# Third layer: step size in the exponent of the decays within chunks, the plain transposed tile by ScalarE, the decays over the sum by broadcast DMA

## The reference, cut to what matters

```
proj = x @ W_in.T + b_in;  gate, hBC, dt = split(proj)
hBC = silu(conv4(hBC));  h, B, C = split(hBC)
dt = softplus(dt + dt_bias);  h = h * dt;  Adt = -exp(A_log) * dt
A_cum = cumsum(Adt within a chunk)
M = (C B^T) * exp(A_cum[l] - A_cum[s]),  s <= l
Y_diag = M @ h
states = recurrence over chunks of (B * exp(A_cum[-1] - A_cum))^T h
Y_off = (C @ states) * exp(A_cum)
y = Y_diag + Y_off + D * hBC_h;  g = y * silu(gate)
out = rmsnorm(g) * norm_w @ W_out.T + b_out
```

## Time and profile before

| what | value |
|---|---|
| median of three runs | 1292.9 us (1292.6 to 1293.01) |
| the profiled execution's own time | 1296.16 us |
| its span | 1294.4 us |
| mean granted TensorE clock | 0.961 |
| busy: TensorE matmul, VectorE, ScalarE, GpSimd | 89%, 73%, 61%, 44% of the span |
| preparation of the third layer's mixer | about 597 to 655 us from the span's start |
| its loop, first to last L1606 | 667.1 to 1103.7 us |

### The profile page before, as it was taken

One profiled execution on the slowest core, in us unless ns is written; L12 is line 12 of the kernel. 1 busy time (PEld: TensorE's weight loads), 2 busy tenths in 40 slices (PEclk: granted clock), 3 DMA queues, 4 the chain that ended last, 5 costly groups with the idle time before them and its releaser, 6 DMA issues.

```text
span 1294.4 us, 14453 instructions
## 1 busy us (share of the span) xinstructions
PE 1150.9 (89%) x4948; PEld 615.3 (48%) x4948; DVE 939.9 (73%) x1361; ACT 795.5 (61%) x1089; POOL 573.9 (44%) x310
## 2 busy tenths in 40 slices
PE   5777999999989999998489999999999999797887
PEld 1332344444344444444266666666666666322554
DVE  4667999999955545345689999998999999323354
ACT  4567666767543334226668888888888888335542
POOL 9002899898816756230014544554454455300000
PEclk8889999999989999898699999999999999798999
DMA  3001555555422111100000000000000000000000
GB/s 121 1 1 58 192 197 178 191 180 180 174 105 82 50 41 41 41 21 0 2 15 15 15 21 15 15 22 15 15 14 22 16 15 8 1 0 1 1 1 33
DMA packets 31111, 68.48 MB, mean 53 GB/s; under 512 B 6101, under 2 KB 12022, under 8 KB 30774
## 3 DMA queue, kind: packets, MB, share of 16 engines
q1 hardware_dynamic: 31038, 67.56, 16.1%
HBM read 65.25 MB, written 1.51 MB: 52 GB/s over the span
## 4 chain that ended last, share of the span: by engine, by line
PE 41%; DVE 30%; ACT 15%; issue 7%; POOL 6%; DMA 1%; DVEq 0%; SPq 0%; POOLq 0%; ACTq 0%
DVE work L1542 7%; DVE work L1561 6%; DVE work L656 4%; PE ps L1006 4%; PE ps L1196 4%; PE ps L1022 3%; PE ps L1014 3%; POOL work L717 3%; ACT work L1403 3%; DVE yd L1606 3%; ACT work L1398 3%; PE ps L1237 2%; DVE work L1609 2%; PE ps L437 2%; ACT ps L553 2%
## 5 line engine op out<-in xcount | busy, mean ns | idle before, releaser
L1670 POOL TENSOR_TENSOR ssum<-ssum,rs 128x1024 f32<-128x1024 f32 x32 | 77.1, 2410 | 221.3 <-DVE work L1542 219.0
L656 DVE TENSOR_TENSOR_SCAN work<-ps,work 128x1024 f32<-128x1024 f32 x64 | 146.6, 2291 | 8.3
L1542 DVE SCALAR_TENSOR_TENSOR work<-work,w_t 128x1024 f32<-128x1024 f32 x96 | 123.3, 1285 | 24.0 <-ACT work L1403 21.7
L437 PE MATMUL ps<-work,ident 128*128 128x512 f32 x256 | 121.7, 598 | 5.6 <-POOL work L717 5.4
L996 POOL TENSOR_TENSOR work<-work,ssum 128x1024 f32<-128x1024 f32 x32 | 76.2, 2388 | 110.1 <-DVE work L1085 57.7
L1085 DVE TENSOR_TENSOR work<-work,ps 128x512 f32<-128x512 f32 x64 | 43.8, 687 | 99.8 <-PE ps L1014 99.8
L553 ACT ACTIVATE ps<-work,A 128x1024 f32<-128x1024 f32 x64 | 71.6, 1118 | 72.4 <-DVE work L656 72.3
L1064 ACT ACTIVATE work<-ps 128x512 f32<-128x512 f32 x64 | 38.1, 597 | 115.4 <-PE ps L1006 115.4
L717 POOL TENSOR_TENSOR work<-work 128x1024 f32<-128x1024 f32 x42 | 99.1, 2362 | 13.6 <-DVE work L656 12.3
L1678 POOL TENSOR_TENSOR yd<-yd,work 128x896 f32<-128x896 f32 x32 | 67.1, 2097 | 70.7 <-DVE work L1609 70.7
L1585 DVE SCALAR_TENSOR_TENSOR work<-work,ps 128x64 f32<-128x64 f32 x384 | 79.4, 275 | 6.3
(11 more groups left out here) (347 smaller groups left out, 2587.5 us busy)
## 6 DMA issues: line engine op xcount, KB each, us to landing
work<-bc_rows SPq DMA_DIRECT2D x42, 512.0 KB, 3.5
yd<-bc_rows SPq DMA_DIRECT2D x22, 512.0 KB, 3.6
...
shared<-in_f SPq DMA_DIRECT2D x3, 512.0 KB, 6.1
...
```

Of the source, the lines that this page charges most:

```text
L437: mm = pe.matmul(ps[:, YACC + h, :], ident[:, :], HS[u % 4][:, h * BL:(h + 1) * BL], start=(n == 0), stop=(n == DS - 1))
L656: dve.tensor_tensor_scan(h, flat_pair(DABANK), h, 0.0, ALU.mult, ALU.add).then_inc(m0["scan"], 1)
L1542: c = dve.scalar_tensor_tensor(HC[u], HP[:, tap:tap + SEQ], par(u, "taps", tap), HC[u], ALU.mult, ALU.add)
L1670: pool.tensor_tensor(ssum[:, b, :], ssum[:, b, :], rs[:, :, :].rearrange("p k t -> p (k t)"), ALU.add).then_inc(m2["ss"], 1)
```

## The change

1. The factor DT of `HDT` goes into the exponent. `LNDT` = ln(DT + 1e-30) is made by ScalarE (one Ln of 128x512). The transposed sums of the start get a second set of 32 rows: ln(DT) minus the cumulative sum, from two more matmuls per chunk (`LNDT` by the identity, `ADT` by `fall`). The set is split into three bf16 parts like the first (64 partitions at a time); the negated copy goes away. The exponentials within chunks then give the decay times the step size. The clamp at 1.0 in `mask_and_weigh` becomes one at 1e30.
2. `HDT` is now the plain transposed tile; ScalarE copies it out of PSUM (`turned_out`, two copies of 128x512 within `exponentials`), and VectorE's `weigh` makes `HDD` alone.
3. `spread_sums` and `decays_out` go away. At the start ScalarE takes exp of the sums (`decay_rows`, 32x512, four times), SP stores them to DRAM (`sdo_rows`) and loads each head's row broadcast over its 64 partitions into Y (`load_decays`, two DMAs of 64x896 per tile). The bf16 parts go through DRAM as well (`arg_rows`), which makes three DMAs of `load_rows` out of four.

The diff, without declarations of semaphores and lines that only build or clear constants (`fall` is minus `upper`, `tiny` is 1e-30, `sel2` is gone):

```diff
@@ -139,16 +139,19 @@
         zero = sb("zero", [P, P])
+        fall = sb("fall", [P, P])
+        parts_lo = sb("parts_lo", [2 * H2, T], BF16)
+        LNDT = sb("lndt", [P, NT, H2])
         sel = selectors[0:96, :, :]
-        sel2 = sb("sel2", [96, H2, P2], BF16)
         eps_t = sb("eps_t", [P, 1])
+        tiny = sb("tiny", [P, 1])
@@ -222,6 +225,8 @@
         share_rows = nc.dram_tensor("share_rows", [E, T], F32, kind="Internal").ap()
+        arg_rows = nc.dram_tensor("arg_rows", [2 * H2, 3, T], BF16, kind="Internal").ap()
+        sdo_rows = nc.dram_tensor("sdo_rows", [H2, T], F32, kind="Internal").ap()
@@ -1123,7 +1128,7 @@
         BT, GT = tiles(5), tiles(6)
-        nparts = slot(7)[0:96, 0:T // 2].bitcast(BF16)
+        split = [parts[0:2 * H2, :], slot(7)[0:2 * H2, 0:T // 2].bitcast(BF16), parts_lo[:, :]]
@@ -1169,25 +1174,57 @@
                 here = slice(b * SEQ, (b + 1) * SEQ)
+                rows = (m2["rows0"], m2["rows1"])[n % 2]
+                pair = arg_rows[H2 + 2 * t:H2 + 2 * t + 2, :, here].rearrange("h k (c l) -> (h k) c l", l=P)
+                sp.dma_start(arg_w[ROW0:ROW0 + 6, n % 2, :, :], pair).then_inc(rows, 16)
                 for h in range(2):
-                    of_head = slice(2 * t + h, 3 * H2, H2)
-                    r = ROW0 + 3 * h
-                    rows = (m2["rows0"], m2["rows1"])[n % 2]
-                    sp.dma_start(arg_w[r:r + 3, n % 2, :, :], nparts[of_head, here].rearrange("k (c l) -> k c l", l=P)).then_inc(rows, 16)
-                    sp.dma_start(arg_m[r + 6:r + 9, n % 2, :, h, :], parts[of_head, here].rearrange("k (c l) -> k c l", l=P)).then_inc(rows, 16)
+                    r = ROW0 + 6 + 3 * h
+                    sp.dma_start(arg_m[r:r + 3, n % 2, :, h, :], arg_rows[2 * t + h, :, here].rearrange("k (c l) -> k c l", l=P)).then_inc(rows, 16)
+            def store_rows(b):
+                sp.wait_ge(m2["dve"], m2["parts"] + (b + 1) * NB // BATCH)
+                here = slice(b * SEQ, (b + 1) * SEQ)
+                for k in range(3):
+                    sp.dma_start(arg_rows[:, k, here], split[k][:, here]).then_inc((m2["rows_out0"], m2["rows_out1"])[b], 16)
+            def store_decays(b):
+                sp.wait_ge(m2["sdo"], (b + 1) * NB // BATCH)
+                here = slice(b * SEQ, (b + 1) * SEQ)
+                sp.dma_start(sdo_rows[:, here], rtf[0:H2, here]).then_inc((m2["rows_out0"], m2["rows_out1"])[b], 16)
+            def load_decays(n):
+                b, t = divmod(n, CT)
+                if n >= 2:
+                    sp.wait_ge(m2["outp"], n - 1)
+                    sp.wait_ge(m2["sqr"], n - 1)
+                for h in range(2):
+                    sp.dma_start(Y[n % 2][h * P2:(h + 1) * P2, P:],
+                                 sdo_rows[2 * t + h:2 * t + h + 1, b * SEQ + P:(b + 1) * SEQ].to_broadcast([P2, SEQ - P])).then_inc(
+                                     (m2["sdo_in0"], m2["sdo_in1"])[n % 2], 16)
             load_tile(1)
+            store_rows(0)
+            store_decays(0)
             sp.wait_ge(m2["rows_const"], 1)
-            sp.wait_ge(m2["act"], m2["neg"] + NB)
+            sp.wait_ge(m2["rows_out0"], 64)
             load_rows(1)
+            store_rows(1)
+            store_decays(1)
+            load_decays(0)
+            load_decays(1)
+            sp.wait_ge(m2["rows_out1"], 64)
             for n in range(CT * BATCH - 2):
+                if n >= 1:
+                    load_decays(n + 1)
                 load_rows(n + 2)
+            load_decays(CT * BATCH - 1)
@@ -1205,7 +1242,7 @@
                 if 0 in quarters:
-                    pe.wait_ge((m2["rows0"], m2["rows1"])[u], 64 * (n // 2 + 1))
+                    pe.wait_ge((m2["rows0"], m2["rows1"])[u], 48 * (n // 2 + 1))
@@ -1222,14 +1259,6 @@
 
-            def spread_sums(n, b, t):
-
-                pe.wait_ge(m2["L"], 4 * n + 4)
-                for h in range(2):
-                    mm = pe.matmul(ps[:, BACK + h, :], sel2[:, 2 * t:2 * t + 2, :].rearrange("k a p -> k (a p)"),
-                                   parts[:, b * SEQ + h * BL:b * SEQ + (h + 1) * BL], start=True, stop=True)
-                mm.then_inc(m2["sdo_mm"], 1)
-
@@ -1245,7 +1274,7 @@
             def within_chunks(n):
-                pe.wait_ge(m2["sdo"], n + 1)
+                pe.wait_ge(m2["hdt"], 2 * n + 2)
@@ -1324,8 +1352,13 @@
             pe.wait_ge(m2["bc_pad"], 2 * NB)
+            pe.wait_ge(m2["act"], m2["lndt"] + 1)
+            pe.wait_ge(m2["rows_const"], 1)
             for i in range(NT):
-                mm = pe.matmul(ps[0:H2, 4 + i // 4, (i % 4) * P:(i % 4 + 1) * P], ADT[:, i, :], upper[:, :], start=True, stop=True)
+                here = slice((i % 4) * P, (i % 4 + 1) * P)
+                pe.matmul(ps[0:H2, 4 + i // 4, here], ADT[:, i, :], upper[:, :], start=True, stop=True)
+                pe.matmul(ps[H2:2 * H2, 4 + i // 4, here], LNDT[:, i, :], ident[:, :], start=True, stop=False)
+                mm = pe.matmul(ps[H2:2 * H2, 4 + i // 4, here], ADT[:, i, :], fall[:, :], start=False, stop=True)
@@ -1410,6 +1442,13 @@
 
+            def turned_out(n, k):
+                act.wait_ge(m2["hdd"], 2 * n + k + 1)
+                if k == 0 and n >= 1:
+                    act.wait_ge(m2["ydiag"], n)
+                act.activation(HDT[:, k * BL:(k + 1) * BL], ps[:, FRONT + k, :], ACT.Copy).then_inc(m2["hdt"], 1)
@@ -1417,6 +1456,8 @@
                         act.activation(ST[:, 0, :], four(MID)[:, 0, :], ACT.Copy).then_inc(m2["first_state"], 1)
+                    if q >= 2:
+                        turned_out(n, q - 2)
@@ -1426,18 +1467,15 @@
 
-            def decays_out(n, u):
-                act.wait_ge(m2["sdo_mm"], n + 1)
-                if n >= 2:
-                    act.wait_ge(m2["outp"], n - 1)
-                    act.wait_ge(m2["sqr"], n - 1)
-                act.activation(Y[u][:, P:], flat2(BACK)[:, P:], ACT.Exp).then_inc(m2["sdo"], 1)
-
                 act.activation(rs[:, :, :], wide(Y[u]), ACT.Square).then_inc(m2["sqr"], 1)
+            def decay_rows(k):
+                act.wait_ge(m2["mid"], k + 1)
+                act.activation(blk(rtf[0:H2, :], k), ps[0:H2, 4 + k, :], ACT.Exp).then_inc(m2["sdo"], 1)
@@ -1450,19 +1488,19 @@
             act.activation(ADT, ADT, ACT.Ln, bias=1.0).then_inc(m2["act"], 1)
+            act.wait_ge(m2["dve"], m2["dt"] + 1)
+            act.activation(LNDT[:, :, :], DT, ACT.Ln, bias=tiny[:, :]).then_inc(m2["act"], 1)
             act.activation(CDEC, ps[:, 2, :].rearrange("p (i h) -> p i h", h=H2), ACT.Exp).then_inc(m2["act"], 1)
-            for k in range(NB):
-                act.wait_ge(m2["pe"], m2["cumT"] + 1)
-                act.activation(blk(parts[0:32, :], k), ps[0:H2, 4 + k, :], ACT.Copy).then_inc(m2["act"], 1)
-                act.wait_ge(m2["mid"], k + 1)
-                act.activation(blk(parts[32:64, :], k), part_tmp[0:H2, k % 2, :], ACT.Copy).then_inc(m2["act"], 1)
+            act.wait_ge(m2["pe"], m2["cumT"] + 1)
+            for k in range(NB):
+                act.activation(blk(split[0], k), ps[0:2 * H2, 4 + k, :], ACT.Copy).then_inc(m2["act"], 1)
+                if k >= 1:
+                    decay_rows(k - 1)
+            decay_rows(NB - 1)
             pad_h(0, 0)
-            for k in range(NB):
-                act.wait_ge(m2["dve"], m2["parts"] + k + 1)
-                act.activation(blk(nparts, k), blk(parts, k), ACT.Copy, scale=-1.0).then_inc(m2["act"], 1)
@@ -1472,7 +1510,6 @@
             def step(n, b, t, u):
-                decays_out(n, u)
@@ -1526,13 +1563,12 @@
             for k in range(NB):
-                r, tb = rs[0:H2, k % 2, :], part_tmp[0:H2, k % 2, :]
-                dve.wait_ge(m2["act"], m2["hi_mid"] + 2 * k + 1)
-                own(dve.tensor_tensor(r, ps[0:H2, 4 + k, :], blk(parts[0:32, :], k), ALU.subtract))
-                dve.tensor_copy(tb, r).then_inc(m2["mid"], 1)
+                r = rs[0:2 * H2, k % 2, :]
+                dve.wait_ge(m2["act"], m2["hi"] + k + 1)
+                own(dve.tensor_tensor(r, ps[0:2 * H2, 4 + k, :], blk(split[0], k), ALU.subtract))
+                dve.tensor_copy(blk(split[1], k), r).then_inc(m2["mid"], 1)
                 dve.wait_ge(m2["mid"], k + 1)
-                dve.wait_ge(m2["act"], m2["hi_mid"] + 2 * k + 2)
-                dve.tensor_tensor(blk(parts[64:96, :], k), r, tb, ALU.subtract).then_inc(m2["dve"], 1)
+                dve.tensor_tensor(blk(split[2], k), r, blk(split[1], k), ALU.subtract).then_inc(m2["dve"], 1)
@@ -1565,9 +1601,7 @@
                 product(HDD, DEC, 0, m2["hdd"])
-                product(HDT, DT, 0, m2["hdt"])
                 dve.wait_ge(m2["tr"], 2 * n + 2)
-                product(HDT, DT, 1, m2["hdt"])
@@ -1604,7 +1638,7 @@
                 dve.scalar_tensor_tensor(YD[:, :], HC[u], vec[:, VCOL["d2"] + t:VCOL["d2"] + t + 1], flat2(BACK), ALU.mult, ALU.add).then_inc(m2["yd"], 1)
-                dve.wait_ge(m2["sdo"], n + 1)
```

(5 more changed lines are left out.)

24 lines of the change are left out of this document (12 added, 12 removed).

## The result

| | before | after |
|---|---|---|
| median of the runs | 1293.0 us (1292.6 to 1295.9, 5 runs) | 1299.7 us (1298.7 to 1300.4, 5 runs) |
| profiled execution, its span | 1296.16, 1294.4 us | 1298.69, 1297.0 us |
| loop, first YD to last YD | 436.60 us | 445.95 us |
| one of the 28 plain tiles, YD to YD, mean | 14.02 us | 14.33 us (13.96 to 14.86) |
| tile 0, tile 16, last interval | 15.73, 16.50, 11.76 | 15.95, 16.94, 11.76 |

The ratio is 1.0041 with a 95% interval of 1.0023 to 1.0059. The prediction was 1282.1 us, in a range of 1277 to 1288, with a chance of 0.93 of faster; it was wrong in sign and by 17.6 us.

The account below looks back on a forecast made before the run. Two nearly level rings of waits, one through VectorE, TensorE and ScalarE, were taken to bound the kernel; loop -11.5 and way in +0.7 gave -10.8, so 1292.9 - 10.8 = 1282.1 us, range 1277 to 1288.

Parts of the forecast that it names:

- The queue of SP: SP's DMAs in the loop: five a tile become six, everything lands within 8 us, so costed at nothing.
- The landing time: Loop DMAs: the nearest row, a 512 KB broadcast, lands in 3.6 us; the two new broadcasts are 458 KB together.
- The slower rival: In the loop, Y* waits for the late broadcast of the decays: +50 us, 1343; chance 0.03.
- The loop's two rings: Chains of waits through VectorE and through TensorE, again level at 13.6 to 13.7 us a tile; loop -11.5 us.
- The rival of dear copies: ScalarE's copies in the loop take 0.69 us each, a tile 13.9, in all 1289 us; chance 0.07.
- The rival of the lower clock: TensorE falls to 1.2 GHz in the loop, standing still before project_h: more than 200 us; chance 0.01.
- The way in: Preparation ahead of the loop: +3.9 us for matmuls, -3.2 for what follows, +0.7 us in sum.
- The 48 matmuls of the sums: TensorE's cumulative sums at the start: 16 become 48, only neighbours overlap, 7.6 us, +3.9.
- The rule of the Trainium skill: No overlap among the start's matmuls, since all use the same rows: +7.4 for +3.9, 1285.6 us; chance 0.14.
- The split: Splitting the sums into three bf16 parts at the start: 8.06 us instead of 11.04, -3.0.
- The transposes: TensorE's transposes at the end of the way in: reached after 8.8 us instead of 9.0.
- tile 0's own step: Before the 31 intervals: tile 0's convolution no longer waits 0.76 us for pad_h, -0.76 us.

Follow-up runs that it names:

- experiment 1: Changed kernel with load_tile(n + 2) put ahead of load_decays(n + 1) in SP's loop, nothing else: 1275.1 us, ratio 0.9826.
- experiments 1 and 2: The second of these: changed kernel with load_tile behind the same wait for sum_out but ahead of the two broadcasts: 1274.5 us, ratio 0.9812.
- experiment 4: Changed kernel with a third broadcast of 64x896, into a place that nobody reads, ahead of load_tile: 1366.0 us, ratio 1.0538.
- experiment 7: Experiment 1 with ScalarE's order changed, first_state ahead of the third exponential: 1277.2 us, ratio 0.986.
- experiment 6: Kernel before with only HDT by ScalarE's copies (turned_out) instead of VectorE's two products; spread_sums and decays_out stay: 1304.9 us, ratio 1.0064.

## Why the prediction was wrong, step by step

**The queue of SP: this step failed.** The prediction said "The weights are wanted by project_h 18 us after that wait" and costed the new order at nothing. The 18 us count one tile too many. `load_decays(n + 1)` waits for the `sum_out` that ends 0.9 us behind YD of tile n; `load_tile(n + 2)` behind it serves `project_h(n + 2)`, which stands at the **start** of step n + 1, 5.28 us after the same YD. The weights are wanted 4.4 us after the wait, not 18. The order needs 1.15 us of issue, 3.6 to 4.5 us of landing and 0.14 us, so 4.9 to 5.8: it is short by 0.5 to 1.4, and the plain tiles are 0.85 us longer in the mean than in experiment 1, 28 times. What hid the load before was that it was issued one period earlier, at 5.64 us after YD (915.33 against 909.69). Its use came at 5.93 us after the next YD, 14.03 + 5.93 - 5.64 = 14.3 us later. The prediction wrote down that the load would be "issued now some 11 us later", and did not ask what was left of 14.3. The subtraction leaves 3.3 us for a landing that takes 3.6 or more.

**The landing time.** I took one for all: "the nearest row, a broadcast of 512 KB, lands in 3.6 us". That was near for the broadcasts (3.7; the two are 448 KB in the page's count, not 458), but the load was taken as independent of what stands ahead of it. It lands in 2.4 or 2.5 us with no broadcast ahead (experiments 1 and 2), in 4.0 behind two, 4.1 behind one and 4.4 behind three. DMA: Bandwidth & Descriptors (Queues, rings and completion order) in the Trainium skill says that SP's queue has one ring on each of the DMA engines, and that each engine consumes descriptors in the order of its ring. By that rule a load behind a broadcast would start later. The landing times bear this out in direction. Their sizes do not grow with the bytes ahead, since one broadcast of 224 KB costs 1.7 us and the third 0.4.

**The slower rival** had the right queue and the wrong consumer. It priced Y* waiting for the decays from 14 us on. In no trace does Y* wait for a DMA; the load behind the decays is late long before. Its chance of 0.03 was that of the wrong victim. A rival per DMA behind the new wait (load, rows, decays), each with its own consumer and distance, would have found it.

**The loop's two rings** were right in kind and somewhat long in size; the change hid them, experiment 1 shows them.

| term | forecast | experiment 1 |
|---|---|---|
| two exponentials end, after YD | 3.57 | 3.57 |
| first copy ends | 4.09 | 4.06 |
| third exponential ends | 4.63 | 4.55 |
| recur starts | 4.94 | 4.77 |
| recur to convolution | 4.83 | 4.86 |
| project_h starts | 5.46 | 5.28 |
| plain tile | 13.62 | 13.48 |

ScalarE's pieces of 128x512 out of PSUM begin 0.47 to 0.49 us behind each other, plain copy and exponential alike; I had 0.52 and 0.54, from a row of three exponentials, and took 0.48 for the lower end. VectorE idles 1.28 us before recur, released by L1458, as foretold (1.5). Tile 0 took 14.96 (forecast 15.73 - 0.6 = 15.1), tile 16 16.94 (16.50 + 0.7 = 17.2), the last 11.76 (11.76 + 0.17 = 11.93). From first to last YD experiment 1 is 15.5 us shorter than before; the forecast had 10.9 there. (Its terms add up to 11.7, not to the 11.5 that it gives, and 0.76 of them lie ahead of the first YD.) The rival of dear copies falls.

**The rival of the lower clock** was nearer than its chance of 0.01. In the plain tiles of the changed kernel the clock stays at 1.00. Behind the first YD it does not: there TensorE waits 2.26 us, and from the end of this wait the lower level holds for 3.4 us. TensorE after, the window, and the same place in experiment 1, whose clock stays at 1.00:

```profile
665.98 1.11 PE L1259 MATMUL ps<-ident,work 128*128 128x128 f32 x4 [2.26 <-ACT work L1443]
```

```profile
665.80:669.20 3.40, 3.22 (x15) 2.85 (x16) 2.28 (x4) 2.99 (x5) 2.03 (x1) 0.50 0.01 2
```

```profile
668.27 0.66 PE L1259 MATMUL ps<-ident,work 128*128 128x128 f32 x4 [2.26 <-ACT work L1443]
```

That is the 1.0 us by which tile 0 is longer than in experiment 1 (15.95 against 14.96). In experiment 4 it costs 1.7 us in each of 14 tiles, and tile 16 of experiment 7 is 2.2 us longer with it. So the mechanism exists in this loop, at waits of some 2 us, and its price is 1 to 2 us a time, not the 200 us of a fall that lasts.

**The way in** was right. Window and timeline after:

```profile
620.00:622.00 2.00, 2.00 (x21) 1.74 (x21) 1.38 (x2) 1.15 (x2) 0.00 (x0) 0.64 0.00 0
```

```profile
627.93 1.07 ACT L1499 ACTIVATE parts<-ps 64x512 bf16<-64x512 f32 x2 [5.18 <-PE ps L1361]
...
635.65 7.75 DVE L1407 SCALAR_TENSOR_TENSOR work<-work,vec 128x1024 f32<-128x1024 f32 x6
...
644.64 3.65 PE L1370 MATMUL ps<-ident,work 128*128 128x128 f32 x16 [4.18 <-ACT work L1506]
```

The 48 matmuls of the sums run from 620.07 to 627.93, 7.86 us against 3.72 before: +4.1, forecast +3.9. Some of it is the clock of 0.64 in the window at their start, a mix of 1.2 and 2.4 GHz. In experiment 1, with the same code, the clock is 1.00 all through and they take 7.22 us:

```profile
623.46:630.68 7.22, 7.22 (x98) 7.02 (x98) 1.38 (x2) 2.00 (x4) 0.00 (x0) 1.00 0.00 0
```

At a clock of 1.00 a piece of three matmuls (six instructions) takes 0.435 us, which is four times the 0.109 us at which L1328 started one instruction behind the other before (32 of them in 3.68 us with the last one's end). So these pieces do share time, and two of six instructions are hidden, as the forecast had it. The rule of the Trainium skill in TensorE: Matmul & The Clock Gate (Part 3, What overlaps and what doesn't) that I set against it, which gave +7.4, is not borne out here. The split takes 635.65 - 627.93 = 7.72 us instead of 11.04, -3.3 for a forecast of -3.0. The transposes follow 9.0 us later, as before (forecast -0.2).

From the start of the first batch's convolution to the first YD it is 57.6 us instead of 56.8, +0.8, where the forecast had about 0 (+0.7 for the preparation, -0.76 at tile 0's own step; that -0.76 is in the trace). The same code takes 56.3 us in experiment 1, -0.5, and 56.2 to 57.6 in the other kernels that have it; what differs among these traces is where the stretches of lower clock fall. The preparation of before took 56.8 us there and 58.5 in experiment 6. So the way in agrees with the forecast as far as these traces can tell, which is about 1.5 us.

**The sum with the one step mended.** By my own terms a plain tile of 14.33 instead of 13.62 is 28 x 0.71 = 19.9 us more, so +9 instead of -10.8. Measured by the traces: -15.5 (experiment 1) + 28 x 0.85 + 1.0 at tile 0 = +9.3, which is the 9.35 us that the loop grew. Nothing is left over in the loop. The 1.0 at tile 0 is the clock's, the 28 x 0.85 are the queue's. Against the forecast of -10.9 from first to last YD the queue adds 23.9 and the clock 1.0, and the loop's own rings, shorter than forecast, take 4.6 off.

**Open** is why one broadcast ahead slows the load as much as two, and what sets TensorE's clock behind the loop, where two profiles differ by 4.4 us. The runs here settle neither.
